# The two opening blocks of a decoder layer become one block without loops, with convolution taps over two PSUM banks

## The chip, the core and the metric

The kernel runs on one core of a Trainium2 chip. The metric is the device time of one execution in microseconds (us), lower is better; the median of several runs is given. The core has a matrix engine (TensorE, PE in the rows), a vector engine (VectorE, DVE), a scalar engine for activation functions (ScalarE, ACT), a general engine (GpSimd, POOL), and a queue that issues transfers from memory (SyncE, SP). They work at the same time, and wait for each other with semaphores.

## What is computed

The reference is one decoder layer on x of 16 sequences x 128 tokens x 256 features: a state-space mixer, a cross-attention and a feed-forward net, each followed by adding the input and a layer norm. The change lies wholly in the mixer's opening part:

```python
proj = x @ in_proj_w.T
gate, hbc, dt = jnp.split(proj, [I, I + CD], axis=-1)      # I = 4096, CD = 6144
conv = conv_general_dilated(hbc_t, conv_w, padding=[(K - 1, 0)], feature_group_count=CD)   # K = 4 taps
hbc = silu(transpose(conv) + conv_b)
hs, B, C = jnp.split(hbc, [I, I + G * N], axis=-1)         # G = 8 groups of N = 128 channels
dt = jax.nn.softplus(dt + dt_bias)
A_cum = jnp.cumsum(-jnp.exp(A_log) * dt)
Y_diag = einsum(C, B, exp(segsum), X)                      # needs C.B for each group and sequence
```

The opening part computes three things that the rest of the mixer reads: the high and low halves of x (`xh`, `xl`), the steps `dt` with their cumulated decays (`ncum`, `cumT`), and for each of the 8 groups the products of B and C of every sequence (`gs`).

## The kernel before

The kernel is one program in stages. `decays`, `bc_groups`, `state_space`, and then attention and the feed-forward net each open a block: all engines meet at a barrier between two blocks. Engines run their lists in order; nothing reorders them.

`decays` (L40 to L162) loads ten small tensors and then the transposed input `xT` in 4 pieces of 512 tokens. PE multiplies `xT` with the weights of the steps into `z_ps` (L98, 16 sequences x 2 halves of the features, each in two passes in the rows). ACT copies `xT` to `xh` (L116), DVE subtracts to get `xl` (L136), and then DVE, ACT and PE turn about: z, |z|, Exp, Ln, dt, da, the cumulated sum by a matrix of ones (L102), three bfloat16 parts of it, their transposes (L105), and `cumT` (L162).

`bc_groups` (L165 to L326) works through 8 groups j. A group has 8 units u: B or C (i = u // 4), times 4 pieces of 512 tokens. A unit is: six matmuls of 128 x 512 (two feature halves, times high x high, high x low, low x high) into one of 4 banks `raw_ps` (L219); the first tap with its bias by ACT into `bc` (L260); the three shifted taps by DVE, each a multiply-add that reads the bank and adds to `bc` in place (L324); the gate Silu by ACT in place (L292). Units of a group before yield products (L231): 4 matmuls, one per sequence, in two passes each, into one of 2 banks `g_ps`, which ACT copies to `gs` (L268). The group's weights are loaded by SP (L200), split by ACT (L253, `w_bc_hi`) and DVE (L307, `w_bc_lo`). The loops are run-time loops over 4 turns of two groups, so the products of group j - 1 run in group j, and the program goes one unit beyond the last one.

`state_space` (L328 on) starts with loads of its first weights `w_raw`, `wo_raw`, the norm weights and `acc` (L410 to L414); ACT splits the weights (L501), DVE sets four constants (L548 to L551) and then computes `wo` and `w_lo` for four heads (L558, L561), and PE starts its first projection (L431) after the first of these.

## Time and profile before

| what | value |
|---|---|
| median of 3 runs | 2318.32 us (2317.78 to 2320.51) |
| the profiled execution: its own time, its span | 2319.96 us, 2318.2 us |
| PE busy | 1922.3 us, 83% of the span |
| DVE busy | 1726.6 us, 74% |
| ACT busy | 1615.0 us, 70% |
| POOL busy | 508.7 us, 22% |
| mean granted clock of TensorE | 0.792 of full speed |
| `decays` | 0 to 41.04 us |
| `bc_groups` | 41.04 to 211.44 us |

The shares of busy time are means over the whole program. What the change can bring is read from the first 220 us, engine by engine. A row of a timeline begins with its start and its length in us; the bracket at its end is the time for which the engine had stood idle, and who ended that.

### The profile page before, as it was taken

The page shows a single profiled execution, that of the slowest core. Times are in us where ns is not written, and L with a number is a line of the kernel's source. Part 1 is how long each engine was busy: PE and PEld are TensorE (multiplying, and loading weights), DVE is VectorE, ACT ScalarE, POOL GpSimd, SP SyncE. Part 2 cuts the span into 40 slices and gives each one's busy share as a digit, 9 for nine tenths or more (in the row PEclk, how much of TensorE's full clock was granted, in tenths as well). Part 3 has the DMA queues.
Part 4 walks back from the last instruction along what each step waited for, and adds up shares of the span by engine and source line. Part 5 has one row for each costly group of instructions (what it writes and reads, how often), then busy time and mean ns, then how long its engine had stood idle before and what let it go on. Part 6 is the DMA issues. An engine that isn't in the chain of part 4 may idle for free. (4 is left out here: it accounts for less than half of the span.)

```text
span 2318.2 us, 41124 instructions
## 1 busy us (share of the span) xinstructions
PE 1922.3 (83%) x11979; PEld 1246.3 (54%) x12044; DVE 1726.6 (74%) x2947; ACT 1615.0 (70%) x2550; POOL 508.7 (22%) x418
## 2 busy tenths in 40 slices
PE   5886999999999999999676777777777777775999
PEld 4665778787878787777553222222222222222787
DVE  3996676767676768777886888888888888886433
ACT  2775888888888888888367777777777777774211
POOL 0000455555555555555100000000000000002001
PEclk9997999999999999999897555555555555555999
DMA  2002000000000000000103988888887888887000
GB/s 61 14 14 91 1 1 26 27 0 27 0 27 0 27 0 27 0 27 0 59 1 64 156 154 154 154 154 154 154 154 152 154 154 154 152 156 156 10 10 19
DMA packets 558410, 164.98 MB, mean 71 GB/s; under 512 B 535072, under 2 KB 550816, under 8 KB 558368
## 3 DMA queue, kind: packets, MB, share of 16 engines
q1 hardware_dynamic: 558368, 164.44, 35.0%
q8 instruction: 24, 0.39, 0.1%
q14 instruction: 18, 0.15, 0.0%
HBM read 28.09 MB, written 2.10 MB: 13 GB/s over the span
## 5 line engine op out<-in xcount | busy, mean ns | idle before, releaser
L1233 ACT ACTIVATE levels<-s_ps,nb,qstep 128x1024 int16<-128x1024 f32 x512 | 611.8, 1199 | 234.0 <-DVE nb L1173 234.0
L1162 DVE TENSOR_REDUCE mx<-s_ps 128x1 f32<-128x512 f32 (+1 forms) x768 | 660.8, 868 | 90.4 <-PE s_ps L1108 82.1
L1108 PE MATMUL s_ps<-kT,qT 48*128 48x512 bf16 x1024 | 520.8, 610 | 231.4 <-ACT levels L1233 230.0
L588 DVE SCALAR_TENSOR_TENSOR xs<-x_ps,cw,xs 128x508 f32<-128x508 f32 (+2 forms) x393 | 291.2, 741 | 174.8 <-ACT xs L510 137.5
L1108 PEld LDWEIGHTS s_ps<-kT,qT 48*128 (+1 forms) x1024 | 82.3, 103 | 480.6 <-issue 458.9
L479 PE MATMUL o_ps<-wo,hid 128*128 x1024 | 243.0, 380 | 4.7 <-DVE acc L575 4.7
L644 POOL TENSOR_TENSOR hid<-y,sg 128x512 f32<-128x512 f32 x128 | 175.3, 1369 | 278.8 <-ACT sg L532 185.9
L1118 PEld LDWEIGHTS ao_ps<-vi,levels_T 128*128 128x128 f16 x4096 | 129.3, 105 | 184.9 <-issue 184.9
L1458 POOL MEMSET minus_half_o<- 128x4 f32 x1 | 0.1, 101 | 994.9 <-POOLq L1051 994.9
L479 PEld LDWEIGHTS o_ps<-wo,hid 128*128 128x128 f32 x1024 | 192.6, 189 | 40.1 <-issue 9.8
L510 ACT ACTIVATE xs<-x_ps,cb,cw 128x512 f32<-128x512 f32 x131 | 101.8, 777 | 117.2 <-PE x_ps L431 117.2
L520 ACT ACT_TABLE_LOAD x130 | 166.8, 1283 | 2.4
L526 ACT ACT_TABLE_LOAD x130 | 166.8, 1283 | 2.4
L1118 PE MATMUL ao_ps<-vi,levels_T 128*128 128x16 f16 x4096 | 152.4, 175 | 6.1 <-DMA levels_T<-levels 6.1
L431 PE MATMUL x_ps<-xh,w_hi 128*128 (+1 forms) x262 | 121.6, 464 | 35.0 <-DVE xs L588 24.3
L324 DVE SCALAR_TENSOR_TENSOR bc<-raw_ps,cw,bc 128x508 f32<-128x508 f32 (+2 forms) x192 | 138.3, 740 | 15.8 <-ACT bc L260 7.8
L520 ACT ACTIVATE decay<-d_ps,ncum 128x128 f32<-128x128 f32 x520 | 148.3, 368 | 1.6
L466 PE MATMUL y_ps<-mix,xdt 128*128 128x128 f32 x1032 | 136.3, 275 | 0.0
L655 POOL TENSOR_TENSOR ssum<-ssum,sq 128x512 f32<-128x512 f32 x96 | 131.3, 1367 | 7.5
L466 PEld LDWEIGHTS y_ps<-mix,xdt 128*128 128x128 f32 x1032 | 125.4, 192 | 0.0
L431 PE MATMUL gate_ps<-xh,w_hi 128*128 (+1 forms) x258 | 113.2, 439 | 0.0
L431 PE MATMUL x_ps<-xl,w_hi 128*128 (+1 forms) x262 | 104.9, 400 | 0.0
(197 smaller groups left out, 3266.4 us busy)
## 6 DMA issues: line engine op xcount, KB each, us to landing
w_raw<-winT_dram SPq DMA_DIRECT2D x18, 512.0 KB, 4.4
wo_raw<-woutT_dram SPq DMA_DIRECT2D x9, 512.0 KB, 5.7
levels_T<-levels SPq DMA_TRANSPOSE x256, 4.3
w_bc<-winT_dram SPq DMA_DIRECT2D x18, 128.0 KB, 2.3
xT<-xT_dram SPq DMA_DIRECT2D x4, 512.0 KB, 8.3
acc<-x_dram SPq DMA_DIRECT2D x1, 2048.0 KB, 11.0
att<-ctxT_dram SPq DMA_DIRECT2D x4, 512.0 KB, 7.4
out_dram<-f_out SPq DMA_DIRECT2D x16, 128.0 KB, 1.7
```

Source lines behind the costliest of these rows:

```text
L324: dve.scalar_tensor_tensor(to[:, :, s:], raw_ps[:, u % BANKS, :, 0:SEQ - s], cw[:, bass.ds(ch, 1), TAPS - 1 - s], to[:, :, s:], ALU.mult, ...
L431: mm = pe.matmul(to[:, :, :], w[:, i, k, h * P:(h + 1) * P], x[:, k, tok], start=(k == 0 and s == 0), stop=(k == KE - 1 and s == 2))
L466: mm = pe.matmul(y_ps[:, b, :], xdt[:, h % 2, b, :], mix[:, h % 2, b, :], start=True, stop=True)
L479: mm = pe.matmul(o_ps[:, b, :], hid[:, h % 2, b, :], wo[:, bass.ds(r // TG % 2, 1), h, :].rearrange("p a e -> p (a e)"), start=(h == 0 and ...
L520: ex = act.activation(decay[:, h % 2, b, :], d_ps[:, b, :], ACT.Exp, bias=ncum[:, bass.ds(r % TG * BG + b, 1), bass.ds(head_of(r, h), 1)])
L526: act.activation(xs[:, h, :, :], xs[:, h, :, :], ACT.Silu).then_inc(xs_ready, 1)
L588: dve.scalar_tensor_tensor(to, x_ps[:, :, 0:SEQ - s], cw[:, head, TAPS - 1 - s], to, ALU.mult, ALU.add).then_inc(chain if s < TAPS - 1 els ...
L644: pool.tensor_tensor(hid[:, hh % 2, :, :], y[:, hh % 2, :, :], sg[:, hh % 2, :, :], ALU.mult).then_inc(hid_ready, 1)
L1108: return pe.matmul(s_ps[:, BANKS[h % 2][chunk], :], qT[0:PARTS * HD, bass.ds(round_, 1), h % NH, :].rearrange("p b t -> p (b t)"), kT[:, h ...
L1118: mm = pe.matmul(o_ps[:, h % NH * HD:(h % NH + 1) * HD], lT[:, s, j, :].bitcast(F16), vi[:, j, h % NH * HD:(h % NH + 1) * HD], start=(j == ...
L1162: dve.tensor_reduce(mx[:, h % 2, at:at + 1], src, AX.XY if what == "cd" else AX.X, ALU.max).then_inc(max_done, 1)
L1233: act.activation(levels[:, s, half * HALF:(half + 1) * HALF].rearrange("p (c k) -> p c k", c=2), s_ps[:, first:first + 2, :], ACT.Exp, bia ...
```

## The change

`decays` and `bc_groups` become one function `front` with one block, without run-time loops. Its unit is a pair p of 0 to 31: group j = p // 4, B or C, and 1024 tokens, that is two banks of one of 3 slots of `raw_ps`. Each first tap, shifted tap and gate is one instruction over 1024 columns; copies of products stay at 512. `z_ps`, `cum_ps` and `ct_ps` share the two banks of `g_ps`. `xT` lies in the memory of `acc`. The low halves of the weights and of the tokens' last two pieces, and three copies, are computed by POOL. The decays' steps are strung between pairs 0 to 5. The first loads of `state_space` are issued when the weights of group 3 are.

```diff
-def decays(nc, mem, io):
...
-def bc_groups(nc, mem, io):
...
+def front(nc, mem, io):
...
+    PAIRS = 4 * G
+    SLOTS = 3
+    WIDE = 2 * BG
...
         wdt = sb("wdt", [P, KE, H])
...
-        raw_ps = ctx.enter_context(nc.psum_tensor("raw_ps", [P, BANKS, BG, SEQ], F32))
-        g_ps = ctx.enter_context(nc.psum_tensor("g_ps", [P, 2, BG, SEQ], F32))
...
+        raw_ps = ps("raw_ps", [P, SLOTS, WIDE, SEQ])
+        g_ps = ps("g_ps", [P, 2, BG, SEQ])
+        z_ps = g_ps[:, 0, :, :].rearrange("p b l -> p (b l)").rearrange("p (b h) -> p b h", h=H)
+        cum_ps = g_ps[:, 1, :, :].rearrange("p b l -> p (b l)").rearrange("p (b h) -> p b h", h=H)
+        ct_ps = g_ps[:, :, :, :].rearrange("p a b l -> p (a b l)").bitcast(BF16).rearrange("p (a c) -> p a c", a=2)
...
+        def pair(p):
+
+            j, q = divmod(p, 4)
+            i, tp = divmod(q, 2)
+            return j, i, tp
...
+                             .rearrange("(k p) t -> p k t", p=P)).then_inc(xt_loaded[tg], 16)
+
+            tokens(0)
+            weights(0)
+            sp.dma_start(mem["cw"][:, :, :], io["conv_w"]).then_inc(taps_loaded, 16)
+            sp.dma_start(mem["cb"][:, :], io["conv_b"]).then_inc(taps_loaded, 16)
+            tokens(1)
+            tokens(2)
+            sp.dma_start(wdt[:, :, :], io["winT"][:, OFF_DT:OFF_DT + H].rearrange("(k p) h -> p k h", p=P)).then_inc(dt_loaded, 16)
+            sp.dma_start(bias[:, :], io["dt_bias"].partition_broadcast(P)).then_inc(dt_loaded, 16)
+            sp.dma_start(alog[:, :], io["A_log"].partition_broadcast(P)).then_inc(dt_loaded, 16)
+            tokens(3)
+            weights(1)
+            for to, of in ((mem["ident"][:, :], io["ident"]), (tri[:, :], io["tri"]), (sel[:, :], io["sel"]),
+                           (maskf[:, :], io["mask"]), (mem["dpar"][:, :], io["D"].partition_broadcast(P))):
+                sp.dma_start(to, of).then_inc(late_loaded, 16)
+            for j in range(2, G):
+                sp.wait_ge(w_ready, j - 1)
+                sp.wait_ge(w_hi_ready, j - 1)
+                weights(j)
+                if j == 3:
+                    sp.wait_ge(hi_ready, TG)
+                    sp.wait_ge(lo_ready[0], 2)
+                    sp.wait_ge(lo_ready[1], 2)
+                    sp.wait_ge(z_done, 2)
+                    for to, of in ((w_raw[:, 0, :, :], io["winT"][:, OFF_X:OFF_X + HG * P]),
+                                   (w_raw[:, 1, :, :], io["winT"][:, 0:HG * P])):
+                        sp.dma_start(to, of.rearrange("(k p) c -> p k c", p=P)).then_inc(mem["ss_w_loaded"], 16)
+                    sp.dma_start(wo_raw[:, :, :], io["woutT"][0:HG * P, :].rearrange("(h p) e -> p h e", p=P)
+                                 ).then_inc(mem["ss_w_loaded"], 16)
+                    sp.dma_start(nw[:, :], io["norm_w"]).then_inc(mem["ss_nw_loaded"], 16)
+                    sp.dma_start(acc[:, :, :], io["x"].rearrange("(b p) e -> p b e", p=P)).then_inc(mem["ss_acc_loaded"], 16)
...
         def _(pe):
-            def raw(n, par, i, tg, bank):
-                pe.wait_ge(conv_done, n + 1)
-                pe.sem_inc(held, 1)
-                for k in range(KE):
...
+            def raw(p):
+                j, i, tp = pair(p)
+                if p % 4 == 0:
+                    pe.wait_ge(w_ready, j + 1)
+                if p >= SLOTS:
+                    pe.wait_ge(conv_done, p - SLOTS + 1)
+                for half in range(2):
+                    tg = 2 * tp + half
+                    if j == 0 and i == 0:
+                        pe.wait_ge(hi_ready, tg + 1)
+                        pe.wait_ge(lo_ready[tg // 2], tg % 2 + 1)
+                    for k in range(KE):
+                        for s, (part, x) in enumerate(((w_hi, xh), (w_hi, xl), (w_lo, xh))):
+                            mm = pe.matmul(raw_ps[:, p % SLOTS, half * BG:(half + 1) * BG, :], part[:, j % 2, i, k, :],
+                                           x[:, k, tg * GT:(tg + 1) * GT],
+                                           start=(k == 0 and s == 0), stop=(k == KE - 1 and s == 2))
...
+            def steps(tp):
+                for b in range(tp * WIDE, (tp + 1) * WIDE):
+                    for k in range(KE):
+                        mm = pe.matmul(z_ps[:, b, :], xT[:, k, b * SEQ:(b + 1) * SEQ], wdt[:, k, :],
+                                       start=(k == 0), stop=(k == KE - 1))
+                mm.then_inc(z_done, 1)
+
+            def products(j, tg):
+                n = j * TG + tg
+                if j == 0:
+                    pe.wait_ge(cum_copied, 1)
+                pe.wait_ge(bc_ready, 4 * j + 3 + tg // 2)
+                if n >= 2:
+                    pe.wait_ge(g_copied, n - 1)
...
-            pe.wait_ge(zeroed, 1)
-            with pe.Fori(0, G // 2) as j2:
-                for par in range(2):
-                    j = j2 * 2 + par
-                    pe.wait_ge(w_ready, j + 1)
-                    for u in range(UNITS):
-                        raw(j * UNITS + u, par, u // TG, u % TG, u % BANKS)
-                        if 0 <= u - G_LAG < TG:
-                            products(j, 1 - par, u - G_LAG)
...
+            for p in range(PAIRS):
+                raw(p)
+                if p < 2:
+                    if p == 0:
+                        pe.wait_ge(dt_loaded, 48)
+                    steps(p)
+                if p == 3:
+                    pe.wait_ge(da_done, 1)
+                    pe.wait_ge(late_loaded, 16 * 5)
+                    pe.matmul(cum_ps[:, :, :], tri[:, :], da[:, :, :], start=True, stop=True).then_inc(cum_done, 1)
+                if p == 5:
+                    pe.wait_ge(parts_done, 1)
+                    pe.wait_ge(ident_ready, 1)
+                    for b in range(BATCH):
+                        tr = pe.transpose(ct_ps[0:PARTS * H, b // 8, (b % 8) * SEQ:(b % 8 + 1) * SEQ],
+                                          parts[:, b, :, :], identb[:, :])
+                    tr.then_inc(ct_done, 1)
+                if p >= 7 and p % 4 == 3:
+                    products(p // 4 - 1, 0)
+                    products(p // 4 - 1, 1)
+                if p >= 8 and p % 4 == 0:
+                    products(p // 4 - 2, 2)
+                    products(p // 4 - 2, 3)
+            for tg in (2, 3):
+                products(G - 2, tg)
...
+            def high(tg):
+                at = slice(tg * GT, (tg + 1) * GT)
+                act.wait_ge(xt_loaded[tg], 16)
+                act.copy(xh[:, :, at], xT[:, :, at]).then_inc(hi_ready, 1)
+
+            def split(j):
+                act.wait_ge(w_loaded[j % 2], 32 * (j // 2 + 1))
+                if j >= 2:
+                    act.wait_ge(raw_ready, 4 * (j - 1))
+                act.copy(w_hi[:, j % 2, :, :, :], w[:, j % 2, :, :, :]).then_inc(w_hi_ready, 1)
+
+            def first_tap(p):
+                j, i, tp = pair(p)
+                ch = H + i * G + j
+                act.wait_ge(raw_ready, p + 1)
+                if j >= 2 and i == 0:
+                    act.wait_ge(g_ready, (j - 2) * TG + TG)
+                act.activation(bc[:, j % 2, i, tp * 2 * GT:(tp + 1) * 2 * GT].rearrange("p (b l) -> p b l", l=SEQ),
+                               raw_ps[:, p % SLOTS, :, :], ACT.Identity, bias=cb[:, ch:ch + 1],
+                               scale=cw[:, ch, TAPS - 1:TAPS]).then_inc(tap_ready, 1)
...
+            def gate(p):
+                j, i, tp = pair(p)
+                act.wait_ge(conv_done, p + 1)
+                at = bc[:, j % 2, i, tp * 2 * GT:(tp + 1) * 2 * GT]
+                act.activation(at, at, ACT.Silu).then_inc(bc_ready, 1)
...
+            high(0)
+            split(0)
+            high(1)
+            act.wait_ge(taps_loaded, 32)
+            high(2)
+            high(3)
+            first_tap(0)
+            for p in range(PAIRS):
+                if p + 1 < PAIRS:
+                    first_tap(p + 1)
+                if p == 2:
+                    act.wait_ge(dt_loaded, 48)
+                    act.activation(expa[:, :], alog[:, :], ACT.Exp).then_inc(exp_chain, 1)
+                    act.wait_ge(abs_done, 1)
+                    act.activation(ez[:, :, :], za[:, :, :], ACT.Exp, scale=-1.0).then_inc(exp_chain, 1)
+                    act.wait_ge(exp_chain, 2)
+                    act.activation(ez[:, :, :], ez[:, :, :], ACT.Ln, bias=1.0).then_inc(soft_done, 1)
+                gate(p)
+                if p % 4 == 1 and p // 4 + 1 < G:
+                    split(p // 4 + 1)
+                if p >= 6 and p % 4 == 2:
+                    copy_products(p // 4 - 1, 0)
+                    copy_products(p // 4 - 1, 1)
+                if p >= 7 and p % 4 == 3:
+                    copy_products(p // 4 - 1, 2)
+                    copy_products(p // 4 - 1, 3)
...
+            def rest_of_weights(j):
+                pool.wait_ge(w_hi_ready, j + 1)
+                if j >= 2:
+                    pool.wait_ge(raw_ready, 4 * (j - 1))
+                pool.tensor_tensor(w_lo[:, j % 2, :, :, :], w[:, j % 2, :, :, :], w_hi[:, j % 2, :, :, :].bitcast(F32),
+                                   ALU.subtract).then_inc(w_ready, 1)
+
+            rest_of_weights(0)
+            for tg in (2, 3):
+                at = slice(tg * GT, (tg + 1) * GT)
+                pool.wait_ge(hi_ready, tg + 1)
+                pool.tensor_tensor(xl[:, :, at], xT[:, :, at], xh[:, :, at].bitcast(F32), ALU.subtract).then_inc(lo_ready[1], 1)
+            rest_of_weights(1)
+            pool.wait_ge(late_loaded, 16 * 5)
+            pool.tensor_copy(identb[:, :], mem["ident"][:, :]).then_inc(ident_ready, 1)
+            pool.tensor_copy(mask[:, :], maskf[:, :]).then_inc(extra, 1)
+            pool.tensor_copy(onehot[:, :, :], sel[:, :].unsqueeze(2).to_broadcast([PARTS * H, H, P])).then_inc(extra, 1)
+            for j in range(2, G):
+                rest_of_weights(j)
...
+            def convolve(p):
+                j, i, tp = pair(p)
+                ch = H + i * G + j
+                dve.wait_ge(tap_ready, p + 1)
+                to = bc[:, j % 2, i, tp * 2 * GT:(tp + 1) * 2 * GT].rearrange("p (b l) -> p b l", l=SEQ)
+                for s in range(1, TAPS):
+                    if s > 1:
+                        dve.wait_ge(conv_chain, p * 2 + (s - 1))
+                    dve.scalar_tensor_tensor(to[:, :, s:], raw_ps[:, p % SLOTS, :, 0:SEQ - s], cw[:, ch, TAPS - 1 - s:TAPS - s],
+                                             to[:, :, s:], ALU.mult, ALU.add).then_inc(conv_chain if s < TAPS - 1 else conv_done, 1)
...
+            step = count(1)
+            for tg in range(2):
+                at = slice(tg * GT, (tg + 1) * GT)
...
+                dve.tensor_tensor(xl[:, :, at], xT[:, :, at], xh[:, :, at].bitcast(F32), ALU.subtract).then_inc(lo_ready[0], 1)
+            dve.wait_ge(taps_loaded, 32)
+            for p in range(PAIRS):
+                convolve(p)
+                if p == 1:
+                    dve.wait_ge(dt_loaded, 48)
+                    dve.wait_ge(z_done, 2)
+                    dve.tensor_tensor(z[:, :, :], z_ps, bias[:, :].unsqueeze(1).to_broadcast([P, BATCH, H]),
...
+                    dve.scalar_tensor_tensor(za[:, :, :], z[:, :, :], -1.0, z[:, :, :], ALU.mult, ALU.max).then_inc(abs_done, 1)
+                if p == 2:
+                    dve.wait_ge(soft_done, 1)
+                    dve.scalar_tensor_tensor(dt[:, :, :], z[:, :, :], 0.0, ez[:, :, :], ALU.max, ALU.add).then_inc(chain, 1)
+                    dve.wait_ge(chain, next(step))
...
+                                             ALU.mult, ALU.mult).then_inc(da_done, 1)
+                if p == 4:
+                    dve.wait_ge(cum_done, 1)
+                    dve.tensor_scalar(ncum[:, :, :], cum_ps, -1.0, None, ALU.mult).then_inc(chain, 1)
+                    next(step)
+                    dve.tensor_copy(parts[:, :, 0, :], cum_ps).then_inc(chain, 1)
...
+                    dve.tensor_tensor(parts[:, :, 2, :], rest[:, :, :], parts[:, :, 1, :], ALU.subtract).then_inc(parts_done, 1)
+                if p == 5:
+                    dve.wait_ge(ct_done, 1)
+                    dve.tensor_copy(cumT[:, :].rearrange("p (a c) -> p a c", a=2), ct_ps[0:PARTS * H, :, :]).then_inc(cum_copied, 1)
...
-            load(0)
-            sp.dma_start(nw[:, :], io["norm_w"]).then_inc(nw_loaded, 16)
-            sp.dma_start(acc[:, :, :], io["x"].rearrange("(b p) e -> p b e", p=P)).then_inc(acc_loaded, 16)
...
-            decays(nc, mem, io)
-            bc_groups(nc, mem, io)
...
+            front(nc, mem, io)
```

What is left out are the removed bodies of `decays` and `bc_groups`, semaphores and names, and the tensors `w_raw`, `wo_raw` and `norm_w`, which are now made outside of `state_space`.

On PE, at the start of the program, `decays` before has the step matmuls as one run, before anything else:

```order
L98 MATMUL z_ps<-wdt,xT 128x32 x32
L102 MATMUL cum_ps<-da,tri 128x512
L105 MATMUL ct_ps<-identb,parts 96x128 x16
L45 UNCONDITIONAL_BRANCH
L212 UNCONDITIONAL_BRANCH
```

After the change (`g_ps` with `wdt` is `z_ps` in the code) the list has the last two matmuls of pair 0, the first half of the steps, and the first matmuls of pair 1:

```order
L162 MATMUL raw_ps<-xl,w_bc_hi 128x512
L162 MATMUL raw_ps<-xh,w_bc_lo 128x512
L170 MATMUL g_ps<-wdt,acc 128x32 [waits fr_dt_loaded]
L170 MATMUL g_ps<-wdt,acc 128x32 x15
L162 MATMUL raw_ps<-xh,w_bc_hi 128x512 [waits fr_lo_ready1,fr_hi_ready]
```

The steps moved from ahead of all projections to between pair 0 and pair 1 (and the other half to between pairs 1 and 2).

On PE, at a group's start after the change, these are the last matmul of pair 4j with j = 2, the products of two pieces, and the first matmul of pair 4j + 1:

```order
L162 MATMUL raw_ps<-xh,w_bc_lo 128x512
L183 MATMUL g_ps<-bc 128x128 [waits fr_g_copied,fr_bc_ready,fr_cum_copied]
L183 MATMUL g_ps<-bc 128x128 x3
L183 MATMUL g_ps<-bc 128x128 [waits fr_g_copied,fr_bc_ready,fr_cum_copied]
L183 MATMUL g_ps<-bc 128x128 x3
L162 MATMUL raw_ps<-xh,w_bc_hi 128x512 [waits fr_conv_done]
```

The last products of the group two before now stand behind the group's first pair.

On ACT, around the end of a group, the list of before runs unit by unit (first tap, gate, copy), with the split of the next weights between:

```order
L260 ACTIVATE bc<-raw_ps,cb,cw 128x512 [waits bc_raw_ready]
L251 ISA
L253 CAST w_bc_hi<-w_bc 128x512 [waits w_loaded1]
L290 REGISTER_ALU
L292 ACTIVATE bc<-bc 128x512 [waits bc_conv_done]
L266 REGISTER_ALU
L268 ISA [waits bc_g_ready]
L268 COPY gs<-g_ps 128x512
```

After the change, from the split of a group's weights on:

```order
L225 CAST w_bc_hi<-w_bc 128x512 [waits fr_raw_ready,fr_w_loaded0]
L233 ACTIVATE bc<-raw_ps,cb,cw 128x1024 [waits fr_raw_ready]
L241 ACTIVATE bc<-bc 128x1024 [waits fr_conv_done]
L245 COPY gs<-g_ps 128x512 [waits fr_g_ready] x2
L233 ACTIVATE bc<-raw_ps,cb,cw 128x1024 [waits fr_g_ready,fr_raw_ready]
L241 ACTIVATE bc<-bc 128x1024 [waits fr_conv_done]
L245 COPY gs<-g_ps 128x512 [waits fr_g_ready] x2
```

The split now stands behind the gate of pair 4j + 1, and the first tap of the next group's first pair waits for products as well as for its own projection.

## Rows read from the trace of the kernel before

**Rows 1.** `bc_groups`: busy us of PE, PEld, DVE, ACT, POOL; then clock, DMA.

```profile
41.04:211.44 170.40, 137.95 (x678) 109.70 (x678) 143.83 (x201) 116.60 (x182) 3.51 (x1) 0.96 0.05 14
```

**Rows 2.** Groups of instructions of the first 212 us, one shape each.

```profile
L260 ACT ACTIVATE bc<-raw_ps,cb,cw 128x512 f32<-128x512 f32 x65 | 50.3, 774 | 4.2 <-PE raw_ps L219 4.1
L324 DVE SCALAR_TENSOR_TENSOR bc<-raw_ps,cw,bc 128x504 f32<-128x504 f32 x64 | 47.5, 743 | 4.1 <-DVE bc L324 1.5
...
L292 ACT ACTIVATE bc<-bc 128x512 f32<-128x512 f32 x64 | 40.4, 631 | 40.8 <-DVE bc L324 39.8
...
L307 DVE TENSOR_TENSOR w_bc_lo<-w_bc,w_bc_hi 128x512 fp32r<-128x512 f32 x9 | 6.2, 693 | 5.1 <-ACT w_bc_hi L253 4.7
L253 ACT CAST w_bc_hi<-w_bc 128x512 fp32r<-128x512 f32 x9 | 5.5, 617 | 14.5 <-POOL bc L300 14.5
L260 ACT ACT_TABLE_LOAD x4 | 5.1, 1283 | 1.9 <-PE raw_ps L219 1.9
```

**Rows 3.** Timeline inside `bc_groups`: taps in a row; one unit and its products.

```profile
64.39 16.41 DVE L324 SCALAR_TENSOR_TENSOR bc<-raw_ps,cw,bc 128x508 f32<-128x508 f32 x22
...
87.88 0.47 PE L219 MATMUL raw_ps<-xh,w_bc_hi 128*128 128x512 f32 x1 [0.57 <-DVE bc L324]
...
89.35 1.05 PE L231 MATMUL g_ps<-bc 128*128 128x128 f32 x8
...
90.16 0.48 PE L219 MATMUL raw_ps<-xh,w_bc_hi 128*128 128x512 f32 x1
```

**Rows 4.** Timeline: products behind idle time of PE; the clock in one stretch.

```profile
77.02 1.13 PE L231 MATMUL g_ps<-bc 128*128 128x128 f32 x8 [1.70 <-ACT gs L268]
...
96.44 2.04 PE L231 MATMUL g_ps<-bc 128*128 128x128 f32 x8 [2.26 <-ACT gs L268]
...
134.97 1.13 PE L231 MATMUL g_ps<-bc 128*128 128x128 f32 x8 [2.31 <-ACT gs L268]
...
96.50:98.00 1.50, 1.50 (x7) 1.50 (x8) 1.47 (x3) 0.81 (x2) 0.00 (x0) 0.50 0.00 0
```

**Rows 5.** Timeline of the start: loads, halves, steps, decays, first projections.

```profile
5.53 1.98 SPq L88 DMA_DIRECT2D xT<-xT_dram  x4
...
12.22 1.04 ACT L116 CAST xh<-xT 128x1024 fp32r<-128x1024 f32 x1 [4.15 <-DMA xT<-xT_dram]
...
12.33 13.84 PE L98 MATMUL z_ps<-wdt,xT 128*128 128x32 f32 x64 [12.33 <-DMA xT<-xT_dram]
...
31.73 2.08 PE L102 MATMUL cum_ps<-da,tri 128*128 128x512 f32 x2 [5.56 <-DVE da L146]
...
36.35 0.69 DVE L158 TENSOR_TENSOR rest<-rest,parts 128x512 f32<-128x512 f32 x1
...
46.40 0.77 PE L219 MATMUL raw_ps<-xh,w_bc_hi 128*128 128x512 f32 x1 [6.90 <-DVE w_bc_lo L307]
...
51.65 0.44 PE L219 MATMUL raw_ps<-xh,w_bc_hi 128*128 128x512 f32 x1
```

**Rows 6.** Groups of later stages: 1024 columns on three engines, and POOL.

```profile
L930 DVE SCALAR_TENSOR_TENSOR rows_q<-q_ps,bq 128x1024 f32<-128x1024 f32 x4 | 4.9, 1223 | 13.3 <-PE parts_T_ps L811 13.3
...
L1233 ACT ACTIVATE levels<-s_ps,nb,qstep 128x1024 int16<-128x1024 f32 x512 | 611.8, 1199 | 234.0 <-DVE nb L1173 234.0
...
L644 POOL TENSOR_TENSOR hid<-y,sg 128x512 f32<-128x512 f32 x128 | 175.3, 1369 | 278.8 <-ACT sg L532 185.9
...
L1466 POOL TENSOR_TENSOR w_up_lo<-w_up,w_up_hi 128x1024 fp32r<-128x1024 f32 x2 | 4.8, 2429 | 0.0
```

**Rows 7.** Timeline from the last unit's end into `state_space`.

```profile
206.73 3.75 PE L231 MATMUL g_ps<-bc 128*128 128x128 f32 x16 [3.71 <-ACT gs L268]
...
210.60 0.59 ACT L268 COPY gs<-g_ps 128x512 f32<-128x512 f32 x1 [1.12 <-PE g_ps L231]
...
212.81 0.48 DVE L551 MEMSET ss_ps<- 128x512 f32 x1
219.25 0.43 DVE L558 TENSOR_TENSOR wo<-wo_raw,norm_w 128x256 f32<-128x256 f32 x1 [5.96 <-ACT w_hi L501]
```

251 lines of the change are left out of this document (47 added, 204 removed).

## The prediction

> **What bounds the kernel now.** The change touches only the first 220 us of a span of 2318.2 us, so I read those stretch by stretch and leave the chain of waits at the program's end alone. First, the busy time of the convolution block [rows 1]: in 170.4 us DVE works 143.8, PE 138.0, ACT 116.6. DVE is the fullest, and PE is close behind it. Second, the groups of instructions [rows 2]: 192 taps of 0.74 us on DVE (64 of each of three widths), and ACT's gates stood idle 39.8 us for DVE. DVE sets the pace. Third, the timeline [rows 3]: 22 instructions (21 taps and one low half) take 16.41 us without a gap, 0.746 each. A unit of six matmuls takes 89.35 - 87.88 = 1.47 us of PE. One piece's products take 90.16 - 89.35 = 0.81, say 0.83 us. At the low clock 16 passes take 3.75 with the end of the last [rows 7], so a piece's 8 some 1.70. The reader should keep three more things from the rows: the pieces ahead of the block (41 us, in which the engines take turns), the hand-over at its end [rows 7], and what PE's clock does behind idle time [rows 4].
>
> **The change, part by part.** The method is to lay the new lists end to end, each instruction starting when its engine is free and its semaphores are there (about 0.1 us for a hand-over), and to follow whoever is last.
>
> *Wide taps.* A tap of 1024 columns does not occur before; the nearest is a multiply-add of that width that reads PSUM, at 1.223 us [rows 6]. The narrow taps, with a scale from memory, cost 0.743 [rows 2]. If the wide one costs one column more per column, as from 0.69 at 512 (the row of 36.35 in [rows 5]) to 1.223, it is 0.743 + 0.53 = 1.27. The other end is two narrow ones, 1.48. I take 1.27, since its nearest row has the engine, the width and the source. A pair's three taps are 3.82 us against 6 x 0.746 = 4.48: 0.66 saved in each of 32 pairs, 21 us. The nine low halves of weights (0.693 on DVE) go to POOL, some 5 us. The first tap becomes 1.20 us (ACT's 1024 columns from PSUM, [rows 6]), the gate 1.05 (the copy at 12.22, [rows 5]). The table loads that the loops repeat (1.283 each, four on L260 in [rows 2]) vanish too, but they lie mostly beside DVE's taps.
>
> *The steady period.* If only DVE counted, a group would take 4 x 3.82 = 15.3 us. PE needs 8 x 1.47 + 4 x 0.83 = 15.1. The chain at a group's end is longer, and it rests on the two orders shown above. From the end of pair 4j - 3's taps: gate 1.0, high half 0.6 [rows 2], low half on POOL 1.4 (512 columns, [rows 6]), PE's pair 4j 2.9, both products that now stand behind it 1.7, their end 0.25, first tap of pair 4j 1.2, hand-overs 0.25: 9.3 us. The tap waits for those products because they still read the `bc` half that it overwrites. DVE has two pairs, 7.6 us, to do in that time. So it stands 1.65 us at each of six group starts, and the group lasts 16.9 us. Before it was about 19.3: from the first projection at 46.40 [rows 5] to the last products at 206.73 [rows 7] are 160.3 us, less some 6 for what lies ahead of the first tap and behind the last one, over eight groups. That is 2.4 us less.
>
> *The start.* Before, the first tokens are issued at 5.53 and used at 12.22 [rows 5]; now ten issues of 0.47 us are gone from ahead of them, and they arrive at about 7. High half 8.0, weights' high half 8.7, POOL's low half 10.1. Pair 0 on PE at the low clock (0.427 us a matmul: 12 between 46.40 and 51.65, [rows 5]) ends at 15.4. First half of the steps: PE's 64 step matmuls took 13.84 us [rows 5], that is 6.9 for a half at the pace they had, and about 3.5 at double pace. The row is the low pace all through. Here each half stands right behind 5.2 us of dense projections, after which the pace doubled at 51.65; so I take one half at each pace, on average 5.2, and keep both ends (3.5 and 6.9) for the range. Pair 1 then ends at 25.8, the second half at 31.0, pair 2 (low) at 36.2, pair 3 (high) at 39.1. First tap of pair 3 ends at 40.5; behind it ACT has Exp and Ln with two table loads, 2 x 1.28 + 2 x 0.63 [rows 2] + 0.3 for a small Exp = 4.1, to 44.5. DVE's dt and da (2 x 0.69) to 45.9, the cumulated sum on PE to 47.6 (it is 2.08 us at low clock, [rows 5]). PE had stood idle, so pair 4 runs low and ends at 52.8; first tap 54.2; taps 58.1; five small DVE steps of 0.43 to 0.69 to 61.3; transposes to 63.0; pair 6 low again to 68.2, first tap, and DVE starts pair 6 at 69.6.
>
> The skill bears on one term here. The Trainium skill, "TensorE: Matmul & The Clock Gate", Part 1, says that the gate opens according to how busy TensorE has recently been; by that the steps, being back to back, should run at the high level. The row of the 64 step matmuls disagrees: PE is busy 13.84 us without a pause and never speeds up. By the page both halves are fast, by the row alone both are slow; the first is the second rival below.
>
> *The rest of the block.* From pair 6 to pair 31 are 25 pairs of 3.82 = 95.5, plus six stalls of 1.65 and 0.3 at the first: DVE starts its last pair at about 174.8, ends it at 178.6. Then gate, the copies of group 6, four products and the last copy: 184.5 at the high clock. PE has stood idle before, and its last products before ran at the low clock (16 passes in 3.75 us, [rows 7]), so 3.0 more (4 x 0.8, one partly hidden). Last, the clock in the middle: PE idles about 2.0 us (16.9 less the 14.9 of its work, 4 x 2.9 and 4 x 0.83) ahead of each group's first pair. Before, idle times of 1.70 left the clock high, of 2.26 brought it to 0.50, of 2.31 did not [rows 4]. A fall costs what it cost there, 0.9 us on the eight passes (2.04 against 1.13) and about as much on what follows until the pace is back, together some 1.6 us. Three of six falls: 4.8 us. The block ends at 184.5 + 3.0 + 4.8 = 192.3, where before the last copy ends at 211.2 [rows 7]: 18.9 us saved.
>
> *The hand-over.* Before, DVE is done with its constants at 213.29 and starts on the weights at 219.25, when the loads have landed [rows 7]. With the loads issued at pair 6 or earlier, DVE goes on at once: 5.96 us. They weigh nothing where they now lie, since SP and the memory are idle in the block (DMA share 0.05, [rows 1]). What follows is unchanged.
>
> Sum: 18.9 + 5.9 = 24.8 us. Against the profiled span: 2318.2 - 24.8 = 2293.4; the profiled execution's own time was 2319.96, 1.6 above the median, so I make it from the median: 2318.3 - 24.8 = 2293.5.
>
> **The rivals.** (1) *Forecast*, 2293.5; chance 0.5. With no fall or with six it is 2288.7 to 2298.3; with the steps at 3.5 or 6.9 each, 3.4 less or more; its own range is 2286 to 2301.
>
> (2) *The start runs at the high clock.* Steps 3.5 each, pairs 1, 2, 4 and 6 at 2.9 instead of 5.2, partly beside DVE: by the same laying end to end the block ends 12.8 us earlier, 2280.7. For it: the dense pair 0; against: PE idles in the decays, and the step rows above. 0.22. (The clock gate page would have it so.)
>
> (3) *A tap over two banks costs two taps*, 1.48: the period goes to 17.8, the block +9.7, 2303. Against it stands the 1.223 row. 0.07.
>
> (4) *The change doesn't do what it says*: POOL's low halves come late (at 2.43 us as for 1024 columns in [rows 6], +7.4, 2301), or the early loads don't help (+5.9, 2299). 0.08.
>
> (5) *The clock falls at every group start* and stays low through pair 4j and the products: 2.24 + 1.74 = 4.0 us in each of six groups, 24.4 in place of 4.8: 2313. 0.07.
>
> (6) *Slower*: the same fall, but low through the next two pairs too. PE was the second engine already; at the low clock a pair costs it 5.2 us against DVE's 3.8. Each further low pair adds 2.24, of which the cover hides a part: 6.7 us a group, 40 in all instead of 4.8, 2329. It decides from 29.6 / 6 = 4.9 us a group on. For it: longer idle times than before; against: before, the first dense projections took the clock back up within 5.2 us [rows 5]. 0.06.
>
> **How the numbers follow.** The median is told from no change within about 0.2%, 4.6 us. Cases 1 to 4 are faster: 0.87. Case 5 is 5 us faster by its price, so near the bound that I count it as same: 0.07. Case 6 slower: 0.06. The range runs from a little below (2), 2278, to between (3) and (5), 2310; outside are (5), (6) and a corner of (2).
>
> **What would show it.** Right: taps of about 1.27 us; DVE starting pair 6 near 70 us; groups of 16.9 us with DVE idle 1.6 us at each group's first pair, released by ACT's first tap, and that one by PE's products; block end near 192; DVE's `wo` directly behind its constants. Wrong: taps near 1.48; POOL's low half above 1.4; granted clock below 0.9 over the block; or a stage behind it that changes its pace, of which nothing is in the sum.

## The result and the profile after

The changed kernel takes 2277.48 us (median of 4 runs, 2276.1 to 2284.15), the kernel before 2318.07 beside it (2317.78 to 2320.51): a ratio of 0.9828, with an interval of 0.9811 to 0.9846. That is 40.6 us less, where 24.8 were forecast; the median lies 0.5 us below 2278, the low end of the range, and by the ratio (0.9828 of 2318.3 is 2278.4) it lies 0.4 us above it. The result is at the very edge of the range, 16 us from the forecast. The profiled execution took 2284.15 us with a span of 2282.2, the longest of its four, so its span is only 36.0 us under that of before.

Where the forecast's steps can be read first is DVE's timeline from pair 6 to the next stage (start, length, engine, line, operation, count, and in brackets the idle time ahead and what ended it). Kernel after:

```profile
60.13 7.65 DVE L308 SCALAR_TENSOR_TENSOR bc<-raw_ps,cw,bc 128x1016 f32<-128x1016 f32 x6 [2.07 <-ACT bc L233]
69.27 15.22 DVE L308 SCALAR_TENSOR_TENSOR bc<-raw_ps,cw,bc 128x1016 f32<-128x1016 f32 x12 [1.49 <-ACT bc L233]
87.66 15.22 DVE L308 SCALAR_TENSOR_TENSOR bc<-raw_ps,cw,bc 128x1016 f32<-128x1016 f32 x12 [3.17 <-ACT bc L233]
104.46 15.22 DVE L308 SCALAR_TENSOR_TENSOR bc<-raw_ps,cw,bc 128x1016 f32<-128x1016 f32 x12 [1.59 <-ACT bc L233]
121.28 15.22 DVE L308 SCALAR_TENSOR_TENSOR bc<-raw_ps,cw,bc 128x1016 f32<-128x1016 f32 x12 [1.60 <-ACT bc L233]
139.68 15.22 DVE L308 SCALAR_TENSOR_TENSOR bc<-raw_ps,cw,bc 128x1016 f32<-128x1016 f32 x12 [3.18 <-ACT bc L233]
156.49 15.21 DVE L308 SCALAR_TENSOR_TENSOR bc<-raw_ps,cw,bc 128x1016 f32<-128x1016 f32 x12 [1.59 <-ACT bc L233]
178.29 0.06 DVE L562 MEMSET ones<- 128x1 f32 x1 [6.59 <-PEq L52]
...
179.57 0.48 DVE L565 MEMSET ss_ps<- 128x512 f32 x1
179.97 0.41 DVE L572 TENSOR_TENSOR wo<-wo_raw,norm_w 128x256 f32<-128x256 f32 x1
```

The row of 60.13 is pairs 6 and 7, that of 69.27 pairs 8 to 11, that of 87.66 pairs 12 to 15, and so on. Each row of 15.22 us is one group, twelve taps without a gap, and each bracket the stall at a group's first pair: 1.49 us in the first, 1.59 or 1.60 in three, and 3.17 and 3.18 in two. From 104.46 to 121.28 is one period, 16.8 us. The last two rows answer to [rows 7]: DVE goes from its constants to `wo` at once, where it waited 5.96 us.

The groups of instructions of the first 178 us, one shape each, give the prices (count, busy us and mean ns, idle time ahead); they answer to [rows 2]. Kernel after:

```profile
L308 DVE SCALAR_TENSOR_TENSOR bc<-raw_ps,cw,bc 128x1016 f32<-128x1016 f32 x32 | 40.7, 1271 | 28.2 <-ACT bc L233 28.2
...
L233 ACT ACTIVATE bc<-raw_ps,cb,cw 128x1024 f32<-128x1024 f32 x32 | 38.6, 1205 | 40.6 <-PE raw_ps L162 25.0 <-PE g_ps L183 15.5
L241 ACT ACTIVATE bc<-bc 128x1024 f32<-128x1024 f32 x32 | 33.8, 1056 | 26.6 <-DVE bc L308 26.6
...
L282 POOL TENSOR_TENSOR w_bc_lo<-w_bc,w_bc_hi 128x512 fp32r<-128x512 f32 x8 | 10.7, 1334 | 127.0 <-ACT w_bc_hi L225 127.0
```

The tap over two banks is 1.271 us against 1.27 put, the first tap 1.205 against 1.20, the gate 1.056 against 1.05, the low half on POOL 1.33 against 1.4.

The chain behind one stall stands in the timeline of all engines ahead of pair 16. Kernel after:

```profile
95.34 1.06 ACT L241 ACTIVATE bc<-bc 128x1024 f32<-128x1024 f32 x1 [1.63 <-DVE bc L308]
96.31 0.60 ACT L225 CAST w_bc_hi<-w_bc 128x512 fp32r<-128x512 f32 x1
...
96.99 1.27 POOL L282 TENSOR_TENSOR w_bc_lo<-w_bc,w_bc_hi 128x512 fp32r<-128x512 f32 x1 [17.12 <-ACT w_bc_hi L225]
...
98.31 0.50 PE L162 MATMUL raw_ps<-xh,w_bc_hi 128*128 128x512 f32 x1 [1.92 <-POOL w_bc_lo L282]
...
101.17 1.95 PE L183 MATMUL g_ps<-bc 128*128 128x128 f32 x16
...
103.22 1.21 ACT L233 ACTIVATE bc<-raw_ps,cb,cw 128x1024 f32<-128x1024 f32 x1 [2.07 <-PE g_ps L183]
...
104.46 1.27 DVE L308 SCALAR_TENSOR_TENSOR bc<-raw_ps,cw,bc 128x1016 f32<-128x1016 f32 x1 [1.59 <-ACT bc L233]
```

Read it downwards: the gate of pair 13, the high half behind it, the low half on POOL, PE's pair 16, the two products behind that pair, the first tap, DVE. From 95.34 to 104.46 are 9.1 us; forecast were 9.3. ACT's first tap is released by `g_ps`, the products, though its own projection had been ready 2 us before. A second chain runs beside this one and, by an estimate, is ready some 0.3 us earlier: the products also need the bank that ACT's copies free, and those start at 100.09 behind the gate of pair 14, so that the first is done at about 100.7, while PE's pair ends at about 101.1.

In the two long stalls the middle of this chain ran at the low level of the clock (a granted clock of 0.50; the high level is 1.00). The windows of PE over pair 12, ahead of the first long stall, and pair 16 (busy time, granted clock, DMA share, GB/s). Kernel after:

```profile
79.90:83.90 4.00, 3.98 (x11) 0.62 0.24 66
98.30:102.00 3.70, 3.69 (x20) 1.00 0.27 71
```

Ahead of both, PE had stood idle the same 1.9 us for the low half.

At the start PE's timeline is this (the rows answer to [rows 5]). Kernel after:

```profile
8.52 0.80 PE L162 MATMUL raw_ps<-xh,w_bc_hi 128*128 128x512 f32 x1 [8.52 <-POOL w_bc_lo L282]
...
12.48 0.44 PE L162 MATMUL raw_ps<-xh,w_bc_lo 128*128 128x512 f32 x1
...
13.45 3.65 PE L170 MATMUL g_ps<-wdt,acc 128*128 128x32 f32 x32
16.94 0.48 PE L162 MATMUL raw_ps<-xh,w_bc_hi 128*128 128x512 f32 x1
...
19.79 4.12 PE L170 MATMUL g_ps<-wdt,acc 128*128 128x32 f32 x32
23.72 0.77 PE L162 MATMUL raw_ps<-xh,w_bc_hi 128*128 128x512 f32 x1
...
38.97 2.07 PE L195 MATMUL g_ps<-da,tri 128*128 128x512 f32 x2 [6.75 <-DVE da L330]
40.06 1.42 PE L162 MATMUL raw_ps<-xh,w_bc_hi 128*128 128x512 f32 x1
...
53.21 1.94 PE L200 MATMUL g_ps<-identb,parts 128*96 128x128 bf16 x16 [5.57 <-DVE parts L343]
54.90 0.78 PE L162 MATMUL raw_ps<-xh,w_bc_hi 128*128 128x512 f32 x1
```

Pair 0's matmuls follow each other at 0.43 us until 12.48 and at 0.23 from then on. The first half of the steps takes 3.65 us, the second 4.12; pair 1 between them is high throughout (16.94 to 19.79). Pair 2, from 23.72, is low for its 12 matmuls: the clock fell during the second half.

Ahead of the first fall the level is read from the distance of the matmuls here, and not from the column of the granted clock. That column prints 1.00 there whatever the pace is. Kernel before, its 64 step matmuls and its first 12 projections, which are 0.43 us apart:

```profile
12.40:26.00 13.60, 13.60 (x64) 1.00 0.15 57
46.40:51.60 5.20, 5.20 (x12) 1.00 0.20 54
```

The changed kernel prints 1.00 over 8.50 to 12.40 as well, and 0.50 over 23.70 to 29.00, with the same 0.43 us between matmuls. So "the low pace" of the steps before is a reading of the pace: 0.216 us a matmul there, 0.11 in the half of 3.65 us.

The block's last copy ends at 178.0 us, against 211.2 before: 33.2 us, and with the 6.0 of the hand-over `wo` starts 39.3 us earlier. In the profiled execution the span gained 36.0, so 3.3 of it were lost again further down; the spans of the other three executions (2274.3, 2274.6, 2276.8) are 5.4 to 7.9 us shorter than this one. That spread was not taken apart.

### The profile page after: what moved, and what is told of

Read it like the earlier page. It is cut to its first block and busy times, and to the rows that moved or that the text cites. A ratio compares the mean times of both kernels' runs of the same rounds, so it can differ in the third digit from the quotient of the medians.

```text
span 2282.2 us, 40123 instructions
## 1 busy us (share of the span) xinstructions
PE 1910.6 (84%) x12006; PEld 1240.5 (54%) x12006; DVE 1695.9 (74%) x2836; ACT 1592.8 (70%) x2475; POOL 525.3 (23%) x430
## 5 line engine op out<-in xcount | busy, mean ns | idle before, releaser
L308 DVE SCALAR_TENSOR_TENSOR bc<-raw_ps,cw,bc 128x1016 f32<-128x1016 f32 (+2 forms) x96 | 119.9, 1266 | 30.5 <-ACT bc L233 28.2
L445 PE MATMUL x_ps<-xh,w_lo 128*128 (+1 forms) x262 | 105.0, 401 | 0.0
```

The costliest lines, as they stand in the source:

```text
L445: mm = pe.matmul(to[:, :, :], w[:, i, k, h * P:(h + 1) * P], x[:, k, tok], start=(k == 0 and s == 0), stop=(k == KE - 1 and s == 2))
```

## The experiments

Each kernel is the changed one with the edit shown, and the kernel before ran beside it. The changed kernel itself, run again with the second set, is the base for these comparisons: 2279.22 us (2277.71 to 2281.25), ratio 0.9829 [0.9812, 0.9845]. Distances below are from its two medians, 2277.48 and 2279.22. The changed kernel did not run beside the last three kernels (`merge_only`, `cum_later`, `products_and_cum`); the kernel before, at 2319.36 there, was 0.5 to 1.3 us above its other medians, so for these the ratios are given too.

> The changed kernel once more, for comparison on the same chip: 2276 to 2284.

**Undo the early loads** (`late_loads`).

```diff
-                if j == 3:
-                    sp.wait_ge(hi_ready, TG)
...
+            load(0)
+            sp.dma_start(nw[:, :], io["norm_w"]).then_inc(nw_loaded, 16)
```

> The changed kernel, with the first loads of state_space issued at that block's start again. My theory: these loads were waited for in full, so DVE's first wo comes some 5.9 us later after its constants than the 0.4 us of the changed kernel, and the time rises by about 5.5 to 6 us, to 2283 to 2284. Rival: the loads were paid for elsewhere (they run beside the projections of pairs 2 to 4); then front itself gets shorter and the time rises by less than 3 us.

Measured: 2283.95 us (2280.46 to 2284.51), 0.9848 [0.9832, 0.9865], 4.7 to 6.5 us above the changed kernel. DVE's timeline at the hand-over, kernel with late loads:

```profile
175.70 0.48 DVE L556 MEMSET ss_ps<- 128x512 f32 x1
184.00 0.43 DVE L563 TENSOR_TENSOR wo<-wo_raw,norm_w 128x256 f32<-128x256 f32 x1 [7.82 <-ACT w_hi L506]
```

The wait of [rows 7] is back, and longer than it was (7.82 against 5.96). In this profile the block also ended 3.9 us earlier than in the changed kernel's (DVE began pair 6 at 56.27 instead of 60.13), so `wo` comes only 4.0 us later (184.00 against 179.97). The rival, that the loads were paid for in the block, would look like this. But the early start goes with the clock: both halves of the steps took 3.65 us and pair 2 was high throughout, and the changed kernel issues the loads only at 34.33, behind all of that. `low_on_dve`, which keeps the early loads, began pair 6 at 55.80. The medians, 4.7 to 6.5 us apart, agree with the forecast's 5.9 and don't fix it closer.

**Undo the wide taps** (`narrow_taps`): six taps of 512 columns a pair, all else as changed.

```diff
+                for half in range(2):
+                    bb = slice(half * BG, (half + 1) * BG)
...
-                    dve.scalar_tensor_tensor(to[:, :, s:], raw_ps[:, p % SLOTS, :, 0:SEQ - s], ...
+                        mm = dve.scalar_tensor_tensor(to[:, :, s:], raw_ps[:, p % SLOTS, bb, 0:SEQ - s], ...
```

> The changed kernel, with each shifted tap as two instructions over one bank (512 columns) instead of one over two banks. Theory: a pair's taps cost 4.48 instead of 3.82 us, and the group's period is two pairs of taps plus the chain of 9.3 us at the group's end, of which DVE hides two pairs: the period rises by 2 x 0.66 and by what the stall still leaves, from 16.8 to about 18.2; the block ends 10 to 11 us later, the time is 2287 to 2289. Rival: DVE's taps bound every pair, so all 32 count, 21 us, 2298. Second rival: PE bounds the block, no change.

Measured: 2290.93 us (2289.85 to 2297.58), 0.9881 [0.9864, 0.9897], 12 to 13 us slower. DVE's timeline, kernel with narrow taps:

```profile
91.78 17.74 DVE L310 SCALAR_TENSOR_TENSOR bc<-raw_ps,cw,bc 128x508 f32<-128x508 f32 x24 [0.66 <-ACT bc L233]
111.43 17.74 DVE L310 SCALAR_TENSOR_TENSOR bc<-raw_ps,cw,bc 128x508 f32<-128x508 f32 x24 [1.91 <-ACT bc L233]
```

The expected 2287 to 2289 was 2 to 4 us short. A group costs DVE 2.5 us more, but the stall shrinks by 0.9 to 1.3: the chain is worked while DVE does two pairs, and longer pairs hide more of it. So the wide tap's 21 us of DVE time were worth some 12 of the kernel's.

**Undo the low halves on POOL** (`low_on_dve`): DVE subtracts them, behind pair 4j + 2 (group 0's at the start).

```diff
-            for j in range(2, G):
-                rest_of_weights(j)
...
+                if p % 4 == 2 and p // 4 + 1 < G:
+                    rest_of_weights(p // 4 + 1)
```

> The changed kernel, with the low halves of the weights on DVE (behind the taps of pair 4j + 2, since before that their high half isn't there) instead of POOL. Theory: the chain at a group's end gets longer, since the low half waits for that pair's taps: from the end of pair 4j + 1's taps it is ready at 3.82 + 0.7 = 4.5 us instead of 3.2, so DVE stalls 1.3 us more in each of six groups less the 0.6 that its own work fills, and it has 0.6 us more work: about 8 us in all, 2285. Rival: only DVE's busy time counts, 8 x 0.61 = 5 us. Second rival: POOL's slower subtraction had cost as much as DVE gains, no change.

Measured: 2289.29 us (2286.22 to 2292.01), 0.9879 [0.9863, 0.9896], 10 to 12 slower. Expected was 2285. DVE's stalls are 2.42 us, and 4.01 where the clock falls, at three groups instead of two. DVE itself pays only 0.6 us a group; the larger part, 6.7 us of stalls in this profile against 4.2 of work, is that the low half now waits for the taps of pair 4j + 2 to end, so that PE stands idle 3.34 to 3.37 us at the first pair of five groups, where it was 1.92.

**Steps ahead of every projection** (`steps_first`), to learn what sets their pace.

```diff
+                if p == 0:
+                    pe.wait_ge(dt_loaded, 48)
+                    for tg in range(TG):
+                        pe.wait_ge(xt_loaded[tg], 16)
+                    steps(0)
+                    steps(1)
                 raw(p)
-                if p < 2:
-                    if p == 0:
-                        pe.wait_ge(dt_loaded, 48)
-                    steps(p)
```

> The changed kernel, with both halves of the step matmuls ahead of pair 0 on PE, as the kernel before has them. In the changed kernel they ran at 3.65 and 4.12 us a half, directly behind dense projections. Theory: the steps do not raise the clock and run at the level that they find; ahead of everything they find the low one and take 13.8 us together (0.216 a pass), and pair 0 follows at the low level. Pair 0's matmuls then start near 26 us instead of 8.5; the time rises by 5 to 10 us, since the steps themselves no longer stand between pairs 0, 1 and 2. Rival: the pace of the steps in the kernel before was due to their loads or to the place of their output; then they take 7.5 us here too and the time is about the same.

Measured: 2286.29 us (2285.11 to 2286.46), 0.9861 [0.9844, 0.9877], 7 to 9 slower. PE's timeline, kernel with the steps first:

```profile
12.23 13.84 PE L170 MATMUL g_ps<-wdt,acc 128*128 128x32 f32 x64 [12.23 <-DMA acc<-xT_dram]
25.88 0.77 PE L162 MATMUL raw_ps<-xh,w_bc_hi 128*128 128x512 f32 x1
...
28.58 0.40 PE L162 MATMUL raw_ps<-xh,w_bc_hi 128*128 128x512 f32 x1
```

The 64 matmuls take 13.84 us, to the hundredth what they took before [rows 5], and behind them the projections start at the low pace. The same instructions behind pair 0 take 3.65 for a half. So the place of their output and the order of the loads, the expectation's rival, were not what made them slow; by themselves, 64 in a row, they ran at the low pace to their end. That they simply run at the level that they find is too much: in eleven profiles with a half behind pair 0, the first half took 3.65 to 4.10 us ten times, also in `split_early` and `narrow_taps`, where pair 0 had been low to its last matmul; only in `merge_only` it stayed low, 6.87 us. In the second half the clock could fall (4.12 in the changed kernel, 4.29 in `narrow_taps`), and the next pair then ran low.

**The high half one gate earlier** (`split_early`), to shorten the chain at its front.

```diff
-                if p % 4 == 1 and p // 4 + 1 < G:
+                if p % 4 == 0 and p // 4 + 1 < G:
                     split(p // 4 + 1)
```

> The changed kernel, with ACT's split of the next group's weights one pair earlier (behind the gate of pair 4j instead of 4j + 1). In the changed kernel DVE stood idle 1.49 to 1.60 us at each group's first pair, or 3.2 where the clock had fallen, and the chain before that is gate, high half, low half, projection, products, first tap. Theory: the weights leave the chain; pair 4j + 4 then starts when its slot is free, and what remains is the products behind it: stall about 1.0, 2 to 4 us gained, and PE's idle time ahead of the pair vanishes, so that the clock doesn't fall: up to 3 us more. Rival: the products' place alone makes the stall: no change.

Measured: 2276.39 us (2272.43 to 2278.31), 0.9821 [0.9805, 0.9838], 1.1 to 2.8 us below the changed kernel, which the intervals don't tell from nothing; expected were 2 to 4, and up to 3 more. The stalls are 1.49 us in the first group and 1.29 in the five others (about 1.0 was expected), and the clock falls in none. The timeline of all engines ahead of pair 12 shows what lasts now. Kernel with the split early:

```profile
80.75 0.40 PE L162 MATMUL raw_ps<-xh,w_bc_lo 128*128 128x512 f32 x1
81.11 1.06 ACT L241 ACTIVATE bc<-bc 128x1024 f32<-128x1024 f32 x1 [1.62 <-DVE bc L308]
82.08 1.05 ACT L245 COPY gs<-g_ps 128x512 f32<-128x512 f32 x2
82.79 2.02 PE L183 MATMUL g_ps<-bc 128*128 128x128 f32 x16 [1.64 <-ACT gs L245]
```

PE's pair is done at 81.15. But PE then stands 1.64 us for the copy that frees the products' bank, which is behind the gate of pair 10. This is the second chain, gate of pair 4j - 2, copy, products, first tap. It was only some 0.3 us shorter than the first, so taking the weights out of the first gave 0.3 us a group. Both chains run through the two products.

**The products out from behind pair 4j** (`products_early`): those of group j - 1 behind pairs 4j + 1 and 4j + 2, ACT's copies behind their gates.

```diff
-                if p >= 7 and p % 4 == 3:
...
+                if p >= 9 and p % 4 == 1:
                     products(p // 4 - 1, 0)
                     products(p // 4 - 1, 1)
-                if p >= 8 and p % 4 == 0:
-                    products(p // 4 - 2, 2)
-                    products(p // 4 - 2, 3)
...
+                if p >= 9 and p % 4 == 2:
+                    products(p // 4 - 1, 2)
+                    products(p // 4 - 1, 3)
```

Group 0's products stay behind pairs 7 and 8. The edit of ACT's copies, left out here, moves them in the same way.

> The changed kernel, with the products of group j - 1 behind pairs 4j + 1 and 4j + 2 on PE instead of 4j + 3 and 4j + 4, and ACT's copies of them behind the gates of 4j and 4j + 1; the split stays where it is. Theory: the first tap of a group no longer waits for products; the chain is 7.6 us, as long as DVE's two pairs, so the stall at the group's first pair goes to about 0, 8 us gained (1.6 in each of six groups, less a little), 2269. Rival: the weights' split alone makes the stall: no change. A stall somewhere else in the group (PE late for pair 4j + 3, behind products that wait for a copy) would show as ACT's first tap of that pair waiting for PE.

Measured: 2265.37 us (2262.87 to 2267.9), 0.9767 [0.9751, 0.9784], 12 to 14 us faster than the changed kernel. DVE's timeline and PE's windows, kernel with the products early:

```profile
94.90 15.22 DVE L318 SCALAR_TENSOR_TENSOR bc<-raw_ps,cw,bc 128x1016 f32<-128x1016 f32 x12 [0.25 <-ACT bc L237]
110.36 15.22 DVE L318 SCALAR_TENSOR_TENSOR bc<-raw_ps,cw,bc 128x1016 f32<-128x1016 f32 x12 [0.25 <-ACT bc L237]
...
165.21 0.06 DVE L572 MEMSET ones<- 128x1 f32 x1 [4.69 <-PEq L52]
```

```profile
60.00:100.00 40.00, 39.12 (x218) 1.00 0.08 21
100.00:160.00 60.00, 56.42 (x310) 1.00 0.02 5
```

The stall is 0.25 us, a period 15.46, and PE is busy 39.1 of 40 us with a granted clock of 1.00. From 178.29 to 165.21 `ones` comes 13.1 us earlier: the stalls sum to 3.3 us instead of 12.6, the tail is 1.9 shorter (4.69 of idle time ahead of `ones` in place of 6.59), and the start of this execution was 2.0 earlier. Expected were 8 us; the falls that no longer happen are 3.2 of the stalls' 9.3, and the earlier start may be no more than the spread. This shows the chain: with the two products gone from between pair 4j and its first tap, and their copies moved with them, 1.34 of the 1.59 us of stall are gone.

**Both of these at once** (`both_early`), the two edits above together.

> Both moves together: the split one pair earlier and the products and their copies as in the kernel with early products. Theory: DVE has its taps back to back, 15.2 us a group, stall 0, PE idle less than 1 us at a time, clock at full speed in the block from pair 6 on: 7 to 11 us less than the changed kernel, 2267 to 2270. Against the kernel with early products alone at most 2 us, by the clock. Rival: PE becomes the bound (14.9 us of work in 15.2) and the gain is less than with early products alone.

Measured: 2270.03 us (2268.2 to 2271.59), 0.9793 [0.9777, 0.981], 4.7 us more than with the products alone. The rival came true: expected were 2267 to 2270, a stall of 0 and at most 2 us on top of the products alone. PE's timeline, kernel with both:

```profile
91.15 2.02 PE L183 MATMUL g_ps<-bc 128*128 128x128 f32 x16 [1.12 <-ACT gs L249]
107.09 2.02 PE L183 MATMUL g_ps<-bc 128*128 128x128 f32 x16 [1.12 <-ACT gs L249]
```

With the split in it, ACT's round at pair 4j is gate 1.05, high half 0.6, two copies 1.05 and the next first tap 1.2: 3.9 us against DVE's 3.82 for a pair. The products behind pair 4j + 1 wait 1.12 us for the copies that free their bank, and DVE stalls 0.70 once a group (with the products alone 0.25), both times at pair 4j + 3. With the products alone that wait is 0.50 us: the split has moved from ahead of the second two copies to ahead of the first two, which these products need, and adds its 0.6 us.

**The merged block alone** (`merge_only`): narrow taps, low halves on DVE and late loads together, which leaves only the decays and projections in one block without loops.

> The changed kernel with its three named parts undone together: taps of 512 columns, low halves of the weights on DVE, and the first loads of state_space at that block's start. What is left is the merged block: slots of two banks with wide first taps and gates on ACT, no run-time loops, decays strung between the pairs, loads in another order. If the three losses measured alone (6, 12 and 10 us) simply add, 2277 + 28 = 2305, 13 us below the kernel before. Theory: taps and low halves both hang on the stall at a group's first pair, and DVE's work, 18.5 us a group, now is what sets the pace; the chain has 9.0 us of cover instead of 7.6, so the low half's delay is partly covered already: 2300 to 2304, 14 to 18 us below the kernel before. Rival: the merge in itself gives nothing, 2318.

Measured: 2318.95 us (10 runs, 2313.99 to 2325.62), 1.0006 [0.9995, 1.0017]. My theory, that the parts would about add up, fell; the merging by itself gives nothing. DVE's and PE's timelines, kernel with the merged block alone:

```profile
63.16 4.50 DVE L294 SCALAR_TENSOR_TENSOR bc<-raw_ps,cw,bc 128x508 f32<-128x508 f32 x6 [2.42 <-ACT bc L221]
...
109.41 0.68 DVE L281 TENSOR_TENSOR w_bc_lo<-w_bc,w_bc_hi 128x512 fp32r<-128x512 f32 x1
110.01 4.50 DVE L294 SCALAR_TENSOR_TENSOR bc<-raw_ps,cw,bc 128x508 f32<-128x508 f32 x6
118.86 13.33 DVE L294 SCALAR_TENSOR_TENSOR bc<-raw_ps,cw,bc 128x508 f32<-128x508 f32 x18 [4.35 <-ACT bc L221]
...
210.91 0.06 DVE L558 MEMSET ones<- 128x1 f32 x1 [8.27 <-PEq L52]
```

```profile
110.15 0.79 PE L150 MATMUL raw_ps<-xh,w_bc_hi 128*128 128x512 f32 x1 [4.60 <-DVE w_bc_lo L281]
```

DVE begins pair 6 at 63.16, 3 us later than in the changed kernel, since the first half of the steps ran low here. But the larger part is that a group takes 21.7 or 22.7 us, more than the 19.3 of before. The low half stands behind 4.5 us of narrow taps, PE is idle 4.60 us for it, and in five of the six groups pair 4j then begins at the low level (7 of its matmuls 0.43 us apart in three groups, all 12 in two; behind the first group's idle time of 1.91 us it did not). So the two undone parts, 12 and 11 us apart, cost some 35 together (40 to 41 less the loads' 6). The profiles say where the surplus is. From DVE's start of pair 6 to its last tap they have 111.6 us in the changed kernel, 123.1 with narrow taps, 121.9 with the low halves on DVE and 139.5 here: 27.9 more, where the two add up to 21.8. Of the 6.1 us over, some 4.4 are falls of the clock. By an estimate that takes the first group's stall, 1.79, for one without a fall, the falls lengthen the stalls here by 9.8 us in all, against 3.2 in the changed kernel, 3.8 with narrow taps and 4.8 with the low halves on DVE. Outside of these stretches the merged block has the later start, which varies by itself, and 8.3 us of idle time ahead of `ones` instead of 6.6.

**The cumulated sum one pair later on PE** (`cum_later`).

```diff
-                if p == 3:
+                if p == 4:
                     pe.wait_ge(da_done, 1)
```

> The changed kernel, with the matmul of the cumulated sum behind pair 4 on PE instead of behind pair 3. In the changed kernel PE stood idle 6.8 us for DVE's da there, with pair 4 queued behind, and DVE then waited 3.5 us for pair 4's first tap. Theory: pair 4 runs at once behind pair 3, DVE's wait of 3.5 us goes, and everything behind shifts by it: 3 to 3.5 us less, 2274. Rival: the clock falls in the longer idle time and pair 5 and 6 give it back: no change.

Measured: 2274.39 us (2270.65 to 2280.28), 0.9818 [0.9797, 0.984], 3 to 5 us faster by the medians, 2.3 to 2.6 by the ratios, and the intervals overlap; 2274 was expected. DVE starts pair 6 at 55.92. PE works on pair 4 while it would have stood 6.75 us for `da`, and the sum then runs in 1.12 us behind 2.58 of idle time instead of 2.07. The latter is no rule: in the next kernel the sum took 2.01 us behind 2.57 of idle time.

**Products early and the sum later** (`products_and_cum`), the two that gained.

> Both orders that helped or should: early products, and the cumulated sum behind pair 4. If they add: 13 us for the products as measured, 3.4 for the sum, 2262 against 2277 to 2279 for the changed kernel. Rival: they meet in the first groups (products of group 0 wait for the decays' copy), and the second gives less than 1 us on top: 2265.

Measured: 2263.5 us (2259.55 to 2267.97), 0.9769 [0.9746, 0.9793], the lowest median of all: 55.9 us under the 2319.36 of before beside it and 14.0 to 15.7 under the changed kernel. Expected was 2262, by the rival 2265. `ones` is at 160.03 us, 5.2 earlier than with the products alone, but the median is only 1.9 lower and the ratio is the same (0.9767 with the products alone), so that no gain of the second order on top of the first is shown.

## Why the prediction came out as it did

**Right, and by its mechanism: the steady period.** The wide tap's price was chosen between 1.27 and 1.48, and is 1.27. The stall was forecast at 1.65 us a group, put on the first tap waiting for the products behind pair 4j; it is 1.59, the trace names `g_ps` as its releaser, and taking the products away takes 1.34 of the 1.59 away. The period of 16.9 us is 16.8. What the forecast didn't have is the second chain, through ACT's copies; it changed nothing here, but it would have shown that an earlier split gives little.

**Right: the hand-over.** 5.9 us forecast; `wo` stands directly behind the constants, and late loads cost 4.7 to 6.5 by the medians.

**Wrong in size: the start.** The failed step is "so I take one half at each pace, on average 5.2", with pair 1 at 5.2 between them. Both halves were at or near the high pace, and so was pair 1, which alone makes 2.3 us of the 9.5. To put pair 1 low also went against the forecast's own premise: 5.2 us of dense matmuls stood ahead of the first half, after which, in the kernel before, the pace had doubled. Against the forecast's times, the lead grows like this:

| event | forecast | measured | lead |
|---|---|---|---|
| pair 0 begins on PE | 10.2 | 8.5 | 1.7 |
| first half of the steps ends | 20.6 | 16.9 | 3.7 |
| pair 1 ends | 25.8 | 19.8 | 6.0 |
| second half ends | 31.0 | 23.7 | 7.3 |
| transposes begin | 61.3 | 53.2 | 8.1 |
| DVE begins pair 6 | 69.6 | 60.1 | 9.5 |

The rest of it is the tokens, which land earlier than put (the high half starts at 5.05 us, not at about 7), and pairs 4 and 6, which are low for about six and four matmuls instead of twelve. The rival of a start at the high clock (2280.7, chance 0.22) is nearer to the result than the forecast, 3.2 us against 16.0, although not all of its start came true: pair 2 and parts of pairs 4 and 6 ran low. In other profiles more of it did: with late loads and with the low halves on DVE both halves took 3.65 us and pairs 1 and 2 were high. And in `merge_only` the halves took 6.87 and 3.66, which is the forecast's one at each pace. So the forecast's start was possible, but not the usual one. `steps_first` shows why neither of the two simple readings holds. The row of before, low all through, was the price of steps that stand ahead of everything; behind a dense pair the same instructions mostly took little more than half. The Trainium skill, "TensorE: Matmul & The Clock Gate", Part 1, lets the level follow how busy TensorE has been; by that, 13.84 us of work without a pause should have raised it, and in two kernels it didn't.

**The other rivals.** Two of the recorded sums have slips that decided nothing: DVE's last pair would begin at 175.3, not 174.8, by the terms named, and the period of rival 3 (17.8) leaves out the stall that the forecast's own chain gives with taps of 1.48 (9.3 + 2 x 4.44 = 18.2; the narrow taps had 18.4). Two-bank taps at 1.48 us, low halves at 2.43 and loads that don't help are ruled out by the rows above. Falls in every group didn't occur in the changed kernel. They do in five of six groups of the merged block alone, behind idle times of 4.60 us, and there they help to eat the whole gain (9.8 us by the estimate above); even so the level was back at the latest behind the pair, so the two further low pairs of the slower rival were seen nowhere.

**Wrong in size: the falls and the tail.** Three falls at 1.6 were forecast; there were two, at 1.58, and with the smaller stall all six come to 12.6 us instead of 14.7. The last products were put at the low clock; here 32 passes took 3.92 us, the high pace (the 16 ahead of them were low, 3.62 us at a granted clock of 0.53, but began at 169.63, beside DVE's last taps), and the tail from DVE's last tap (171.70) to the last copy is 6.3 us instead of 8.9. Together with the start: 9.5 + 2.1 + 2.7 = 14.3, which is the block's end at 178.0 instead of 192.3.

**Open.** 24.8 + 14.3 are 39.1 us, and the median fell by 40.6. The difference is within the spread of the runs. What decides whether an idle time of 1.9 us ahead of pair 4j is followed by the low level (at two of five group starts here, in the second run of the kernel, with late loads and with the steps first, at none with the cumulated sum later, whose middle is the same) was not found; the experiments only show that where PE's idle times in the groups were 1.64 us or less, in four kernels, it didn't happen. Nor was it settled how the start's clock varies: in the profiles of six kernels with this start and wide taps, pair 6 began between 56.3 and 60.5 us. This spread of 4 us in single executions is as large as what `cum_later` and `split_early` gained.

## What to carry to other kernels

When a change speeds up the fullest engine, price the chain that crosses from one round to the next, and look for work on it that merely stands in the queue between two links: here two products behind pair 4j cost 1.6 us a group and, moved two slots earlier, gave as much as the wide taps did. Look also for a second chain just below the longest one: it decides what shortening the first can give. Undoing two parts one by one doesn't give what both are worth: together they made PE idle long enough that its clock fell at five group starts of six. Undo them together too. And a row taken at a low clock prices the clock, not the instruction: before it goes into a sum, ask what the engine did ahead of it.

## What the runs showed of the hardware

- The PE clock: 64 matmuls of 32 columns kept PE busy for 13.84 us and stayed at the low pace (in two kernels). Behind a dense pair 32 of them took 3.65 to 4.29 us in 21 halves of eleven profiles, and 6.87 once: they mostly ran at the high level and sometimes lost it on the way.
- The column of the granted clock printed 1.00 over matmuls 0.43 us apart ahead of the first fall, and 0.50 over the same spacing later (windows above).
- PE idle for 1.9 us was followed by the high level at three group starts and by the low one at two, with the same instructions on both sides (windows above: 1.00 and 0.62). Behind 3.34 to 3.37 us it was low at three of five (`low_on_dve`), behind 4.60 at five of five (`merge_only`).
- POOL's subtraction of 128x512 took 1.27 us beside DVE's taps, and 1.78 us at 6.69 us, where DVE subtracted the low half of the tokens (from SBUF, 1.22 us) at the same time. DVE's twelve taps took 15.22 us with a subtraction on POOL beside them and 15.21 without (the last row of taps above).
